# Node-type columns kept as bfloat16 in five words of a gathered row, and transposed by a bfloat16 matmul

## The reference, cut to what matters

```python
h = maximum(layernorm(x), 0)
k, q, v = type_proj(h, W) + b            # one of three 128x128 matrices, by the node's type
att = (q[dst] * rel_att[edge_type](k[src])).sum(-1) * rel_pri / sqrt(dk)     # 8 heads
aggr = segment_sum(softmax_by_dst(att) * rel_msg[edge_type](v[src]), dst)
x = x + layernorm(sigmoid(skip) * (gelu(aggr) @ Wa + ba) + (1 - sigmoid(skip)) * h) * ln_g + ln_b
h = maximum(layernorm(x), 0)
x = x + graph_conv(graph_conv(h))        # relu(D_in^-1/2 A D_out^-1/2 h W + b), twice
```

## Time and profile before

| what | value |
|---|---|
| three executions | 2852.10, 2852.71, 2857.18 us |
| the profiled execution's own time | 2854.7 us |
| its span, first to last instruction | 2853.0 us |
| mean granted TensorE clock over the span | 0.777 |
| busy share of the span: PE, DVE, ACT, POOL | 65%, 72%, 41%, 58% |
| instructions | 48,869 |
| DMA, mean over the span | 131 GB/s |

### The profile page before, as it was taken

How to read it: one execution, slowest core, us unless ns; L and a number is a source line. 1 busy time by engine, 2 the same in 40 slices (tenths; PEclk the granted TensorE clock), 3 DMA queues, 4 the chain that set the end, 5 groups by cost and what they waited for, 6 DMA issues and landing times. The chain is left out here.

```text
span 2853.0 us, 48869 instructions
## 1 busy us (share of the span) xinstructions
PE 1866.8 (65%) x12706; PEld 1449.3 (51%) x12706; DVE 2062.4 (72%) x7060; ACT 1159.7 (41%) x3211; POOL 1655.0 (58%) x1737
## 2 busy tenths in 40 slices
PE   4630001999999999999992677887757763333332
PEld 1100000999999999999992344444435442222221
DVE  7994563999999999999996777777745553333333
ACT  0000001777777777777771345554422221111111
POOL 0002334777777777777761354455467767777776
PEclk9985555999999999999996798899855555555555
DMA  2006774777777777776761344444344442222222
GB/s 52 0 0 202 249 247 134 172 185 184 183 183 184 181 184 185 185 181 184 182 171 33 91 127 123 122 118 124 102 122 132 131 118 72 71 71 70 71 70 52
DMA packets 400270, 374.38 MB, mean 131 GB/s; under 512 B 60254, under 2 KB 342269, under 8 KB 397032
## 3 DMA queue, kind: packets, MB, share of 16 engines
q1 hardware_dynamic: 360856, 276.76, 35.3%
q0 software_dynamic: 31360, 64.76, 10.7%
q10 hardware_dynamic: 7806, 29.98, 2.6%
HBM read 227.43 MB, written 147.13 MB: 131 GB/s over the span
## 5 line engine op out<-in xcount | busy, mean ns | idle before, releaser
L1683 DVE TENSOR_TENSOR_SCAN conv_sT<-keep,conv_sT,conv_pT 128x128 f32<-128x128 bf16 x390 | 187.1, 480 | 384.3 <-PE conv_pT L1658 383.5
L1658 PE MATMUL conv_pT<-ident,conv_row 128*128 128x128 f32 x392 | 182.1, 464 | 405.2 <-ACT conv_row L1643 328.3
L814 POOL DMA_INDIRECT att_xsd<-xt,ends_i x392 | 390.2, 995 | 95.1 <-issue 94.7
L1658 PEld LDWEIGHTS conv_pT<-ident,conv_row 128*128 128x128 f32 x392 | 74.5, 190 | 496.2 <-ACT conv_row L1643 384.9
L995 PE MATMUL att_kvc<-att_hm,w_kv 128*128 128x128 f32 x2352 | 295.9, 276 | 0.0
L939 ACT ACTIVATE att_nhb<-att_nxr 128x128 f32<-128x128 f32 x391 | 168.8, 478 | 276.6 <-DMA att_nxr<-xt 276.6
L995 PEld LDWEIGHTS att_kvc<-att_hm,w_kv 128*128 128x128 f32 x2352 | 279.6, 193 | 0.0
L1368 POOL TENSOR_TENSOR edge_glm<-edge_gl,edge_mask 128x1536 f32<-128x1536 f32 (+1 forms) x56 | 153.1, 2735 | 214.2 <-PE edge_pc L1459 207.4
L1664 PE MATMUL conv_pm<-w,conv_sT 128*128 128x128 f32 x784 | 258.9, 434 | 12.1 <-DVE conv_res L1690 11.0
L1643 ACT ACTIVATE conv_row<-conv_row,ats 128x128 f32<-128x128 f32 x196 | 78.6, 401 | 425.3 <-DMA conv_row<-t,idx 425.3
L1108 DVE TENSOR_TENSOR att_kvm<-att_kvc,att_rel_in 128x1024 f32<-128x1024 f32 x196 | 240.0, 1224 | 13.1 <-PE att_kvc L1008 1.2
(11 more groups left out here) (240 smaller groups left out, 4883.6 us busy)
## 6 DMA issues: line engine op xcount, KB each, us to landing
att_mask_in_t<-type_row SPq DMA_DIRECT2D x196, 192.0 KB
xt<-xr ACTq DMA_DIRECT2D x23, 1224.0 KB
att_nxr<-xt SPq DMA_DIRECT2D x97, 262.0 KB
att_rel_in<-rel_row SPq DMA_DIRECT2D x196, 128.0 KB, 3.2
out_dram<-att_not SPq DMA_DIRECT2D x97, 256.0 KB, 3.8
ta<-att_nhs SPq DMA_DIRECT2D x97, 256.0 KB
xr<-in_x_dram SPq DMA_DIRECT2D x22, 1088.0 KB
xd_rows<-att_xsd SPq DMA_DIRECT2D x196, 65.5 KB, 3.1
```

What stands on the lines that cost most here:

```text
L814: pool.indirect_dma_start(out=xsd[:, v, k, :], out_offset=None, in_=xt, in_offset=bass.IndirectOffsetOnAxis(ap=ends_i[:, n, k:k + 1], axis ...
L1658: nc.tensor.transpose(pT[:, n % 2, 0:P], row[:, n % R], ident[:]).then_inc(t_ready, 1)
L1683: dve.tensor_tensor_scan(sT[:, n % R], keep[:, n * P:(n + 1) * P], pT[:, n % 2, 0:P], before, ALU.mult, ALU.add).then_inc(s_ready, 1)
```

## The change

A row becomes `RW = 140` words, 560 bytes. The nine flags are nine bfloat16 values in words 135 to 139 (ten halves, of which the last is unused); `type_cols` gives the view. POOL sets word 139 of both buffers to zero before the first group, since DVE's `is_equal` writes only nine of the ten halves, and DVE waits once for that. The flags are now written as bfloat16 by L692 and read as bfloat16 by L698. In the attention stage the transpose in float32 is replaced by an ordinary matmul of the bfloat16 flags with `identb`. Stores to `xt`, the gathers and the buffers `xr` and `xsd` are 140 words wide.

```diff
-RW = 144
+RW = 140
...
+def type_cols(rows):
+    return rows[:, :, C_TYPE:RW].bitcast(BF16)[:, :, 0:K9]
...
                 @block.gpsimd
                 def _(pool):
+                    for b in range(2):
+                        pool.memset(xr[b][:, :, RW - 1:RW], 0.0).then_inc(half_set, 1)
                     pool.memset(mh[:], -0.5).then_inc(half_set, 1)
-                    pool.wait_ge(half_set, 1)
+                    pool.wait_ge(half_set, 3)
...
                 @block.vector
                 def _(dve):
+                    dve.wait_ge(half_set, 2)
+
...
-                        dve.tensor_tensor(xr[b][:, :, C_TYPE:C_TYPE + K9],
+                        types = type_cols(xr[b][:])
+                        dve.tensor_tensor(types,
...
-                        dve.tensor_tensor(am[:], xr[b][:, :, C_TYPE:C_TYPE + K9].rearrange("p j (t k) -> p j t k", k=SPLIT)[:, :, :, 0],
+                        dve.tensor_tensor(am[:], types.rearrange("p j (t k) -> p j t k", k=SPLIT)[:, :, :, 0],
...
                             for e in range(2):
-                                m = nc.tensor.transpose(tT[:, e], xsd[:, v, e, C_TYPE:C_TYPE + K9], ident[:])
+                                m = nc.tensor.matmul(tT[:, e], type_cols(xsd[:, v, e:e + 1])[:, 0], identb[:], start=True, stop=True)
                             m.then_inc(types_seen, 1)
```

## The result

Five executions of the changed kernel took 2890.60 to 2896.72 us, median 2892.72. The kernel before was executed twice more beside it, in 2852.69 and 3608.43 us; the second stands alone, has no profile, and leaves its median at 2852.71. The ratio without it is 1.0138, with a 95% interval of 1.0123 to 1.0153: the change makes the kernel slower, by 40.0 us between the medians. The profiled execution after took 2892.72 us, with a span of 2891.0; before it was 2854.7 and 2853.0, so between the two profiles lie 38.0 us.

A forecast was written before the change was run, and what follows sets the result against it. PE was taken to bound the attention stage. From the profiled 2854.7 us, +34.8 for the steps and -1 for the row stage gave 2888.5, or 2886.5 us for the median; range 2829 to 2893 us.

The forecast's parts named there:

- What bounds the stage: Attention stage: PE sets the pace, one step each 5.21 us, with DVE close behind at 4.95 us of work.
- The pair's own price: Attention step: the two flag matmuls fall from 0.11 to 0.056 us each, minus 0.106 us a step.
- Entering border: Attention step: extra time going from float32 matmuls into the new bfloat16 pair, 0.10 us.
- Leaving border: Attention step: extra time going from the new bfloat16 pair to the float32 matmul L1044, 0.19 us.
- Steps: Attention stage: 192 full-pace steps, each 0.18 us longer, +34.8 us in all.
- Why there is a border: Extra time where PE matmuls of two kinds meet: from 9 rows, or from type or used array shape; both paid, 0.47.
- The first rival: Attention stage: only matmuls with 9 contraction rows cost extra, so the kernel ends faster at 2831.3 us; chance 0.36.
- the silent L1034: Attention step: the old float32 flag transpose has 9 columns yet pays nothing extra, argued for the faster ending.
- The row stage: Loop of load, moments, store: 2.8% fewer bytes per store, -1 us.
- The bound of +18: Row stage: stores of unaligned rows slowed to the loads' rate, up to +18 us; 0.03 that it decides the sign.
- Memsets, DVE's wait, L692, L698, gathers, later stages at 0: Row stage's small additions and flag accesses, the hidden gathers and all later stages: no change in time.
- Median against profile: Whole kernel: profiled execution before was 2.0 us above the runs' median, so 2888.5 became 2886.5 us.

The follow-up runs named there:

- E1: Kernel before with the float32 flag transpose L1034 as an ordinary float32 matmul of 9 columns: 2952.14 us.
- E2: Kernel before, 576-byte rows and float32 flags kept, L1034 as a 9-column bfloat16 matmul reading the flags' upper halves: 2888.21 us.
- E11: Kernel before with L1034 as a bfloat16 matmul of 41 stationary columns, 32 words ahead of the flags included: 2893.81 us.
- E3: Kernel before with L1034 as a bfloat16 matmul of 73 stationary columns, 64 words ahead of the flags included: 2844.0 us.
- E4: Kernel before, L1034 untouched, the attention stage's four 9-row bfloat16 matmul lines contracting over 128 rows, 119 of them zero: 2810.5 us, ratio 0.9849.
- E6: Changed kernel with the two bfloat16 flag matmuls in transpose form, into a bfloat16 PSUM tile, still 9 columns: 2893.27 us.
- E5: Changed kernel with rows of 576 bytes again, flags still bfloat16: 2888.23 us.
- E8: Kernel before with E4's 128-row matmuls and E3's 73-column bfloat16 flag matmul together: 2803.03 us, ratio 0.9822.
- E10: E8 with the edge stage's 9-row bfloat16 matmuls over 128 rows as well: 2806.37 us.
- E12: The same kernel as E8, against the kernel before, measured again beside E10: 2807.14 us, ratio 0.9833.

## Why the prediction was right, and where it was off

The forecast was 2886.5 us for the median and 2888.5 for the profiled execution; 2892.7 came for both. It was slower, as forecast. The median lies 0.3 us under the top of the stated range (2829 to 2893), with two of its five executions above that; that it fell inside is luck. The sign had been given 0.56.

- **What bounds the stage**: right. PE was busy 999.6 of 1000 us after, too, and each added ns of a step reached the end (35.3 of steps, 37.9 at the softmax).
- **The pair's own price**, minus 0.106: right. Its two records were 58 ns apart, and its successor came 149 ns behind its second record, of which 56 are its own.
- **Entering border**, 0.10 from the distance L995 to L996: 0.094 (203 - 109).
- **Leaving border**, 0.19 from the last steps of the earlier trace rows: 0.194 (149 - 56 and 213 - 112). Taking L1044's own entry rather than the transposes' (0.14) was what made this right.
- **Steps**: 192 x 0.184 = 35.3 against 34.8. The terms as forecast already give this: 0.10 + 0.19 - 0.106 is 0.184, and the forecast's product is off by the 0.5. That a 9-column shape would cost what the 9-row shape of its rows costs was an assumption, and it held.
- **Why there is a border**: the prediction left it open between the type and the shape, and had the same price for either. It is the shape: E1, E2 and E11 pay and E3 doesn't, E4 takes the borders away by rows. The Trainium skill ("TensorEngine Tiling (Array Packing)", Tiling Modes) says that a change of tiling mode drains TensorE, and lists 128 rows by 32 and by 64 columns, and 32 rows by 128 columns, as modes of their own. What 9, 41 and 73 columns and 9 rows cost agrees with this list; that the lost time is a drain, no run shows. The same page of the Trainium skill, section Restrictions and Gotchas, excludes column tiling for float32 transposes, and E1 against the kernel before, and E6, agree: of the four 9-column forms tried, the float32 transpose alone passes free.
- **The first rival** (only the 9 rows cost, 2831.3 us) fell with the result. Its argument had been the silent L1034. That one is silent since it is a float32 transpose, not since 9 columns are harmless.
- **The row stage** is the step that failed: -1 us forecast, "as a partition's share is one block of 9.5 KB whatever its rows are". +2.4 came. This reasoning held for the stores, which kept their price per byte. It overlooked that the loads write into the same buffer, which the program lays out in rows of 128 words of `x` at the new pitch, and E5 shows that the buffer's or the table's pitch makes these slower. The other term of it, less to store, was there (1.1 points of the queue's share) and was outweighed. The 3.4 us between -1 and +2.4 are most of the 4.2 by which the profiled execution lay above the sum; 0.5 is the product above.
- **The bound of +18** for unaligned rows was taken from stores slowed to the loads' rate. The sign was right; size and queue weren't.
- **Memsets, DVE's wait, L692, L698, gathers, later stages at 0**: right. L692's counterpart took 0.33 us against 0.31 and L698's 0.22 against 0.24, in sum nothing for a group; after the softmax the two traces run in parallel.
- **Median against profile**: I subtracted 2.0 us because the profiled execution before lay so far above its median. After, it lay on the median. That is the remaining 2 us between 38.0 and 40.0, and is within the scatter: beside the experiments, the kernel before had medians of 2853.8 to 2854.8.

## What to carry to other kernels

Where TensorE bounds a stage, read its records start to start around every matmul that uses fewer rows or columns than its neighbours, and count the visits to such shapes, not the matmuls: a visit cost 0.2 to 0.3 us of a 5 us step here, more than a bfloat16 pair could save. Idle columns or zero rows that bring it to the neighbours' shape cost no matmul time in this stage (E4, E8), but then look at once at which engine is next, and at the granted clock, which was lower in E10's edge stage. A denser row is not free either: 3% fewer bytes at a pitch of 560 made the loads beside it slower.

## What was not expected of the hardware

- A float32 transpose with 9 stationary columns stands among 128-column float32 matmuls without a border; the same operands as an ordinary matmul pay 0.09 us on entering and 0.20 on leaving (E1).
- 41 columns pay like 9, and the pair itself is 73 ns apart instead of 57; 73 columns pay nothing (E11, E3).
- Behind a 56 ns bfloat16 matmul a float32 matmul's second record comes 0.05 us late even without a border (E3), and behind a border 0.10 late. This halves what a lone bfloat16 pair can bring between float32 ones.
- Loads of the same packets and bytes took 3 to 5% more queue time into rows of 560 bytes' pitch (38.7% against 37.4 in the kernel before and 37.0 in E5).
- In the edge stage the granted clock fell from 0.87 to 0.78 when little but the rows of a few matmuls changed (E10 against E12, which also lacks three memsets), with PE's busy time the same within 2.3 us.
